# Where the sum of x and its layer norm is made: on VectorE behind the norm, or on GpSimd

## What is computed

```python
# layer 0
x = x + L0_conv(_ln_c(x), ...)     # and L0_conv(h) itself ends in "return h_out + identity", identity = _ln_c(x)
t = _to_tokens(x); t = t + L0_ffn(_ln_t(t), ...)
# layer 1
x = x + L1_conv(_ln_c(x), ...)
t = _to_tokens(x); t = t + L1_ffn(_ln_t(t), ...)
```

## Time and profile before

| | |
|---|---|
| median of 3 runs | 7031.78 us (7015.9 to 7036.94) |
| profiled execution, its own time | 7010.7 us |
| its span | 7008.9 us |
| TensorE busy | 5784.1 us (83%) |
| VectorE busy | 5549.2 us (79%), 9325 instructions |
| ScalarE busy | 4280.4 us (61%) |
| GpSimd busy | 337.2 us (5%), of it 317.7 us the 256 sums of L1001 |
| mean granted TensorE clock | 0.943 |

### The profile page before, as it was taken

How to read it: one execution, slowest core, us unless ns; L and a number is a source line. 1 busy time by engine, 2 the same in 40 slices (tenths; PEclk the granted TensorE clock), 3 DMA queues, 4 the chain that set the end, 5 groups by cost and what they waited for, 6 DMA issues and landing times. The chain is left out here.

```text
span 7008.9 us, 111308 instructions
## 1 busy us (share of the span) xinstructions
PE 5784.1 (83%) x40192; PEld 2345.7 (33%) x40192; DVE 5549.2 (79%) x9325; ACT 4280.4 (61%) x7549; POOL 337.2 (5%) x366
## 2 busy tenths in 40 slices
PE   2788888888898888888888888888888888888875
PEld 0233333333333333333333333333333333333332
DVE  5778887788887778887888888788888878887763
ACT  1456766666766656766666766656766656766654
POOL 1000000000000000000000000000000000000000
PEclk9899999999999999999999999999999999999997
DMA  1223323333323333323333323233323333323322
GB/s 40 60 73 86 87 75 85 79 78 88 89 73 87 78 80 87 88 74 86 79 80 87 89 74 88 76 80 87 89 75 86 81 76 87 89 72 87 79 59 63
DMA packets 395480, 556.44 MB, mean 79 GB/s; under 512 B 71490, under 2 KB 391427, under 8 KB 391771
## 3 DMA queue, kind: packets, MB, share of 16 engines
q1 hardware_dynamic: 394940, 549.32, 31.0%
HBM read 233.66 MB, written 78.68 MB: 45 GB/s over the span
## 5 line engine op out<-in xcount | busy, mean ns | idle before, releaser
L859 DVE SCALAR_TENSOR_TENSOR conv<-mid,w_dw,conv 128x1568 f32<-128x1568 f32 x1536 | 2837.6, 1847 | 28.1
L663 PE MATMUL b_banks<-shifted,w_combo 128*32 128x392 f32 x6144 | 637.4, 539 | 280.6 <-DMA shifted<-g 233.5
L535 PE MATMUL bank<-xc_a,w_exp 128*128 128x392 f32 x1536 | 706.3, 570 | 187.1 <-DVE xc_a L842 120.3
L583 PE MATMUL bank<-conv,w_proj_gated 128*96 128x392 f32 x2048 | 729.8, 499 | 5.9 <-DVE w_proj_gated L871 5.9
L598 PE MATMUL bank<-x,centering 128*96 128x392 f32 x1536 | 655.8, 519 | 92.0 <-ACT phases L722 52.7
L775 ACT ACTIVATE hidden<-b_banks 128x1176 f16<-128x1176 f32 x512 | 590.5, 1153 | 179.0 <-PE b_banks L618 175.8
L782 ACT ACTIVATE hidden<-hidden 128x1176 fp8e5<-128x1176 f16 x512 | 604.5, 1188 | 44.9 <-PE bank L627 24.5
L715 ACT ACTIVATE mid<-bank 128x392 f32<-128x392 f32 x768 | 381.1, 497 | 373.8 <-PE bank L535 350.5
L691 ACT ACTIVATE g<-bank 96x392 f32<-96x392 f32 x512 | 254.0, 496 | 520.9 <-PE bank L598 467.8
L742 ACT ACTIVATE conv<-conv,bn_affine 128x1568 f32<-128x1568 f32 x192 | 324.9, 1692 | 329.1 <-DVE conv L859 328.7
L914 DVE TENSOR_SCALAR hidden<-hidden,b_q 128x392 f16<-128x392 f16 x1536 | 395.0, 313 | 131.1 <-ACT hidden L775 130.8
(11 more groups left out here) (157 smaller groups left out, 7926.6 us busy)
## 6 DMA issues: line engine op xcount, KB each, us to landing
phases_on<-phases SPq DMA_DIRECT2D x768, 101.5 KB, 2.6
shifted<-g SPq DMA_DIRECT2D x512, 149.6 KB, 2.7
r_b<-rstd_row_b SPq DMA_DIRECT2D x512, 147.0 KB, 3.0
shifted<-g SPq DMA_DIRECT2D x256, 199.5 KB, 2.9
x<-in_x SPq DMA_DIRECT2D x32, 1176.0 KB, 7.8
r_a<-rstd_row_a SPq DMA_DIRECT2D x256, 147.0 KB, 2.9
x_plus_norm<-x SPq DMA_DIRECT2D x256, 147.0 KB, 2.6
r_a<-x_plus_norm SPq DMA_DIRECT2D x256, 147.0 KB, 2.3
```

Of the source, the lines that this page charges most:

```text
L535: mm(ring[bank][:, 0:TW], WEXP[:, 128 * k:128 * k + 128], xc_tile(t, 128), start=True, stop=True)\
L583: mm(o, WPS[:, k, :], tile(conv(k, t // NTH, parity), t % NTH, 128), start=(k == 0), stop=False)
L663: last = mm(rows(PB[32 * u:32 * u + 32, m, 0:TW]), WC[:, u // 2, 32 * m:32 * m + 32], SH[t % 2][:, u, :].rearrange("p (h w) -> p h w", w=G ...
L859: v.scalar_tensor_tensor(out=acc, in0=src, scalar=WDW[:, k, j:j + 1], in1=acc, op0=ALU.mult, op1=ALU.add).then_inc(sem["convolved"], 1)
```

## The change

VectorE makes the sum itself, as the second instruction of its own `norm_a` step, behind a wait for the norm that it has just issued. The list `POOL` loses its entry and `gpsimd_steps` its branch. No other step moves: each list of steps is as it was.

```diff
     "POOL": {
-        "norm_a": (4007, 4903, 5096, 5325, 5773, 6384, 8893, 9938), "gn 0": (23979,)},
+        "gn 0": (23979,)},
...
                 v.tensor_tensor(xc_tile(t), xc_tile(t), RA[t % 2][:, :], ALU.mult)\
                     .then_inc(sem["normed_a"], 1)
+                dve.wait_ge(sem["normed_a"], at(NT * n + t + 1))
+                v.tensor_tensor(tile(XA, t), tile(XA, t), xc_tile(t), ALU.add).then_inc(sem["xplus_a"], 1)
...
-            elif name == "norm_a":
-                t = arg[0]
-                pool.wait_ge(sem["normed_a"], at(NT * n + t + 1))
-                g.tensor_tensor(tile(XA, t), tile(XA, t), xc_tile(t), ALU.add).then_inc(sem["xplus_a"], 1)
```

## The result

| | before | changed |
|---|---|---|
| median, us | 7036.17 (7015.9 to 7041.94, 7 runs) | 7062.66 (7050.73 to 7071.13, 7 runs) |
| profiled execution, us | 7010.7 | 7050.73 |
| span, us | 7008.9 | 7048.9 |
| ratio of the times | | **1.0041 [1.0028, 1.0054]** |

The change makes the kernel slower by 0.4%. The forecast was 7064 us, 0.46% slower. The changed kernel was run a second time beside later experiments and gave 1.0048 [1.0032, 1.0065]. A ratio is worked out from all runs of the two kernels and so is not exactly the quotient of their medians.

The account below looks back on a forecast made before the run. VectorE's delay between norm 0 and the gate passes into the projection, where TensorE is full. 31 images by 1.0 us plus 1 us on 7010.7 gives 7043, in the median's terms 7064 us; range 7020 to 7110.

Parts of the forecast that it names:

- The sum costs 0.60 on VectorE: In the norms' stretch, each sum linked to its norm makes the step 1.08 us in place of 0.48.
- Norms 1 and 2 and the gate are relieved, since GpSimd held them: With GpSimd's sum gone, norms 1 and 2 lose 0.33 and 0.55 us, the gate 0.81 and 0.77.
- The rival in which the gate stays long (7112): L866 and L871 are long for another reason; delay 2.57 us an image, 80 us in all; chance 0.08.
- Norm 4 comes 0.32 later: Norm 2 ends 0.32 us later, so norm 4's fetch and norm 4 do too; 0.11 of the wait is left.
- Aggregation +0.92: After sum 4, the group norm's aggregation, and from there its chain and TensorE's 3198.98, come 0.92 us later.
- Aggregation to the end of the gate +0.22 (1.80 for three sums less 1.58): Sums 5 to 7 bring the delay to 2.72 us; less 0.81 and 0.77, L871 ends 1.14 later.
- Projection +1.0 into a full stretch: The first projection matmul starts 1.0 us later an image, opening the stretch in which TensorE is full.
- the rival of 7032 to 7045: An unseen wait in the full stretches takes up the 1.0 us an image; chance 0.12.
- 31 x 1.0 + 1 = 32 us: Whole run: 31 images by 1.0 us, plus an estimated 1 us for the first image's norms.
- Neither rival: TensorE's clock ahead of the projection stays low longer (7091, chance 0.12) or comes back sooner (7006, chance 0.08).
- The unpaid link (7049): A sum's wait for its norm costs nothing, so a sum is 0.48 us, 17 us in all; chance 0.15.
- the gate's relief of 1.58: Without GpSimd's sums, 0.81 us goes in the step from L866 to L871 and 0.77 in L871.

Follow-up runs that it names:

- The experiment meant to settle it by time: Against the changed kernel, each sum became a step of its own, one VectorE instruction later, not directly behind its norm; 1.0029 [1.0019, 1.0040] to the kernel before.

## Why the prediction was right

Taken by its own steps:

- **The sum costs 0.60 on VectorE.** Right to 0.02: 0.56 each in 256 rows, 1.06 for a linked pair, so 0.58 over the norm's own 0.48.
- **Norms 1 and 2 and the gate are relieved, since GpSimd held them.** Right and shown without the change's own edit: the gate by moving GpSimd's sums 6 and 7 off it, the gate and both norms by leaving out the sum. The rival in which the gate stays long (7112) is out. The Trainium skill, SBUF — State Buffer, section "Who interferes with whom", states that VectorE and GpSimd share a pair of ports that one instruction holds exclusively to its end, and names a VectorE instruction with two SBUF inputs against a GpSimd instruction that reads SBUF. The trace agrees for L871, which has two such inputs, 1428 ns against 658. L866 has one, and it was held as well, 976 ns against 156.
- **Norm 4 comes 0.32 later.** By the table it came 0.44 later, with 0.30 of the wait left in the image shown, not 0.11. By the traces norm 2 ends 0.27 later and its fetch is issued 0.03 behind it in both kernels, as the forecast has it. The rest is the fetch itself, 3.30 us from issue to norm 4 before and 3.47 after. It takes 3.40 and 3.48 in two kernels in which GpSimd still makes these sums, so that part is not the change.
- **Aggregation +0.92.** By the table +1.01, over all executions +0.87.
- **Aggregation to the end of the gate +0.22 (1.80 for three sums less 1.58).** By the table +0.14.
- **Projection +1.0 into a full stretch.** By the table +1.05; 28.89 in the image shown, where 28.8 was forecast. It was not taken up elsewhere: the rival of 7032 to 7045 is out by the interval, whose lower end of 1.0028 is 7056.
- **31 x 1.0 + 1 = 32 us.** By medians it was 26, and 32 in the repeat; the ratios are 0.41% and 0.48%, around the 0.46% forecast. The 1 us for the first image can't be seen: its projection opens at 260.8 us before and 260.0 changed. That 7064 and 7062.66 lie so close is luck: before came out at 7036.17 with seven runs where the forecast had started from 7031.8, and that made up for most of a rise that was 6 us smaller.
- **The clock.** Neither rival came: the six expansion matmuls take 4.27 as before in the image shown (4.16 in the mean, 4.14 before) and the eight behind them 2.92. In that image the stretch's mean clock went from 0.76 to 0.82; the forecast had named a clock far from 0.76 as a sign of being wrong. But it is one image: from norm 0 to the projection the mean over 29 is 0.81 before and 0.79 changed.
- **The unpaid link (7049).** Its premise fails in the rows (1.06 against 0.96 for a pair). Its time of 1.0025 lies just under the change's interval. The experiment meant to settle it by time did not.

So the mechanism was right, and not only the number. Two things that stand in the forecast's walk without being said are shown by the experiments. Before the change TensorE's own way in is 0.15 behind the gate, so the gate's relief of 1.58 is worth nothing by itself and pays only for sums that stand in front of it. And it has 0.92 of the 1.0 already at the aggregation, so sums 0 to 4 carry the loss (1.0033 against 1.0005 for the last three).

## What to carry to other kernels

An engine that looks to have room by its share may still sit on the path in one short stretch. Read, at the entrance of the next full stretch, how far each way in lies behind the other (here 0.15 us), since a relief of the one that is not the later can win nothing, and a relief of the later one no more than that. When work must move onto such an engine, its place decides the price. Here the same sums cost 0.4% directly behind their norms. In waits for other engines and behind the instruction that the path was waiting for, they gained 0.4%, with GpSimd's interference gone in both.

## What the runs showed of the hardware that was not expected

A GpSimd addition holds up even tiny VectorE work: 128x5 takes 0.97 us in place of 0.16. GpSimd pays too. With sums 6 and 7 moved behind the gate, beside the depthwise taps, its sums take 1579 ns in the mean (1246 in the kernel before):

```profile
L1003 POOL TENSOR_TENSOR x<-x,xc_a 96x392 f32<-96x392 f32 x256 | 403.1, 1579 | 2362.5 <-DVE xc_a L842 2167.2 <-DVE w_proj_gated L871 195.3
```

A gap of 2.30 us of TensorE in front of a full stretch cost more than itself: the eight matmuls behind it took 4.39 to 4.57 us in place of 2.87 in 22 of 29 images, and gaps of 0.51 and 1.11 at the same place had no such price in any of the 29. The seven images that the 2.30 us gap spared are those in which the clock came back earlier, while the six expansion matmuls of the stretch ran (3.70 to 4.02 us for them in place of 4.20 to 4.27). Why that should spare them is not settled; no run varied what TensorE did ahead of the gap.
